# Attention with the value products two steps behind the exponentials, and the row sums directly behind them

## The reference, cut to what matters

```python
q = jnp.dot(x, Wq).reshape(b, t, H, HD).transpose(0, 2, 1, 3)
scores = jnp.einsum('bhqd,bhkd->bhqk', q, k)
scores = jnp.where(causal[None, None], -jnp.inf, scores)
weights = jax.nn.softmax(scores * (1.0 / HD ** 0.5), axis=-1)
ctx = jnp.einsum('bhqk,bhkd->bhqd', weights, v)
```

## Time and profile before

| | us |
|---|---|
| median of 3 runs | 3003.71 (2999.08 to 3004.33) |
| the profiled execution | 2999.23 |
| its span in the profile | 2997.6 |
| first and last score matmul of the attention (L475) | 360.1 and 1307.8 |
| PE busy, share of the span | 96% |
| DVE, POOL and ACT busy | 43%, 32%, 30% |

### The profile page before, as it was taken

The page is one execution under the profiler, slowest core; times in us unless marked ns, Lnnn a source line. Parts: engine busy times, 40 slices in busy tenths (PEclk is TensorE's granted clock), DMA queues, the critical chain, the costliest instruction groups (busy, mean ns, idle before and its releaser), DMA issues. The chain is left out here.

```text
span 2997.6 us, 43157 instructions
## 1 busy us (share of the span) xinstructions
PE 2863.8 (96%) x17688; PEld 1233.8 (41%) x17688; DVE 1275.0 (43%) x1579; ACT 896.9 (30%) x1599; POOL 969.7 (32%) x553
## 2 busy tenths in 40 slices
PE   6999799999999999989959999999999998999998
PEld 3445333333333333224434444444444444444443
DVE  5334877777877877125642232232233220001001
ACT  3111166666666666740111111121111110000000
POOL 0000066766767667742222222222222221001001
PEclk9999799999999999999979999999999999999999
DMA  4222101011011010022221111111111113223320
GB/s 163 79 74 76 41 1 42 2 42 42 1 42 33 10 28 1 1 78 95 101 56 39 39 45 42 42 41 40 42 42 45 39 34 114 66 66 93 104 66 28
DMA packets 146158, 152.58 MB, mean 51 GB/s; under 512 B 44912, under 2 KB 121200, under 8 KB 146032
## 3 DMA queue, kind: packets, MB, share of 16 engines
q1 hardware_dynamic: 146032, 150.78, 16.7%
HBM read 100.80 MB, written 49.81 MB: 50 GB/s over the span
## 5 line engine op out<-in xcount | busy, mean ns | idle before, releaser
L681 POOL TENSOR_TENSOR c_prob<-c_prob 128x1024 f32<-128x1024 f32 (+1 forms) x288 | 605.1, 2121 | 583.0 <-ACT c_prob L585 579.9
L602 DVE TENSOR_REDUCE c_maxes<-c_s 128x2 f32<-128x1024 f32 (+3 forms) x640 | 648.7, 1059 | 219.8 <-PE c_s L456 113.6
L585 ACT ACTIVATE c_prob<-c_s 128x512 f32<-128x512 f32 (+1 forms) x1152 | 598.0, 571 | 371.8 <-PE c_s L475 187.9
L475 PE MATMUL c_s<-c_q,c_k 97*128 97x512 f16 (+3 forms) x1280 | 365.4, 353 | 8.2 <-DMA c_q<-c_mrow 2.7
L1086 DVE SCALAR_TENSOR_TENSOR e_h<-e_up,e_silu 128x512 f32<-128x512 f32 (+1 forms) x88 | 60.8, 691 | 579.8 <-PE e_up L1048 579.8
L490 PE MATMUL c_ctx<-c_prob,v_sb 128*32 128x512 f32 (+3 forms) x2560 | 294.1, 540 | 0.5 <-ACT c_c L574 0.5
L1135 POOL TENSOR_TENSOR e_hl<-e_h,e_hh 128x512 f16<-128x512 f32 (+1 forms) x88 | 101.9, 1158 | 588.8 <-ACT e_hh L1109 588.8
L1046 PE MATMUL e_gp<-x_hi,e_w_hi 128*128 128x512 f16 (+1 forms) x704 | 267.7, 380 | 2.5 <-DVE e_w_lo L1076 2.5
L1047 PE MATMUL e_gp<-x_lo,e_w_hi 128*128 128x512 f16 (+1 forms) x704 | 267.7, 380 | 0.0
L1048 PE MATMUL e_gp<-x_hi,e_w_lo 128*128 128x512 f16 (+1 forms) x704 | 267.6, 380 | 0.0
L1047 PE MATMUL e_up<-x_lo,e_w_hi 128*128 128x512 f16 (+1 forms) x704 | 266.9, 379 | 0.0
(11 more groups left out here) (141 smaller groups left out, 3212.2 us busy)
## 6 DMA issues: line engine op xcount, KB each, us to landing
h_hi<-e_hh SPq DMA_DIRECT2D x84, 128.0 KB, 1.7
h_lo<-e_hl SPq DMA_DIRECT2D x84, 128.0 KB, 1.8
f_h_hi<-h_hi SPq DMA_DIRECT2D x7, 1344.0 KB, 8.5
f_h_lo<-h_lo SPq DMA_DIRECT2D x7, 1344.0 KB, 6.9
b_x<-L_attn_x SPq DMA_DIRECT2D x16, 512.0 KB, 6.5
c_q<-qk_hi SPq DMA_DIRECT2D x16, 512.0 KB, 6.9
d_x<-L_attn_x SPq DMA_DIRECT2D x16, 512.0 KB, 5.1
x_dram<-d_x SPq DMA_DIRECT2D x16, 512.0 KB, 2.6
```

Source lines behind the costliest of these rows:

```text
L475: last = nc.tensor.matmul(S2[:, h % 2, at:at + w], K[:, g % 2, k * P:(k + 1) * P], Q[:, g % 2, h, b * BANK + q:b * BANK + q + w], start=Tr ...
L585: nc.scalar.activation(prob(g, s, 0, w)[:, h, :], S2[:, h % 2, 0:w], ACT.Exp, scale=exp_scale).then_inc(exp_done, 1)
L602: nc.vector.tensor_reduce(MAXES[:, heads, t, u], S1[:, heads, 0:unit_width(tile)], AX.X, ALU.max).then_inc(maxed, 1)
L681: return nc.gpsimd.tensor_tensor(one, one, two, ALU.add)
```

## The change

Three edits, all in `attend`. Products are issued two steps behind the scores instead of one. The sum pieces of a step are issued directly behind the products, between the two pairs of heads, instead of at the step's end behind the late unit; a piece made from a single step's exponentials gets a wait for these of its own. ScalarE reads a finished context one step later. The close after the last group is reordered to match.

```diff
@@ sums_after
-                    if c is not None:
+                    if c is None:
+                        pe.wait_ge(exp_done, REP * (STEPS * g + a + 1))
+                    else:
                         pe.wait_ge(added, 2 * (len(pairs) * g + pairs.index((a, c))) + half + 1)
@@ order on TensorE
                 for s in range(STEPS):
                     scores(g, s, (0, 1))
-                    if s:
-                        products(g, s - 1)
+                    if s >= 2:
+                        products(g, s - 2)
                     elif g:
-                        products(g - 1, STEPS - 1)
+                        products(g - 1, STEPS + s - 2)
+                    if g:
+                        sums_after(g - 1, s + STEPS)
+                    sums_after(g, s)
                     if more:
                         for tile in early_in[s]:
                             unit(g + 1, tile)
...
-                    if g:
-                        sums_after(g - 1, s + STEPS)
-                    sums_after(g, s)
+            products(GROUPS - 1, STEPS - 2)
+            sums_after(GROUPS - 1, STEPS)
             products(GROUPS - 1, STEPS - 1)
-            for s in range(STEPS, STEPS + 3):
+            for s in range(STEPS + 1, STEPS + 3):
                 sums_after(GROUPS - 1, s)
@@ ScalarE
-                        if s == last_of[b] + 1:
+                        if s == last_of[b] + 2:
                             read_context(g, b)
-                    if g and s == 0:
+                    if g and s == 1:
                         read_context(g - 1, NB - 1)
```

## The result

The changed kernel takes 3075.68 us in the median (3073.37 to 3076.53, 4 runs) against 3004.02 us (2999.08 to 3007.24) before: 1.0239 times, 95% interval 1.0226 to 1.0252, 71.7 us more. 3082 was forecast, with a range of 3058 to 3110.

The account below looks back on a forecast made before the run. TensorE's order bounds steps with units, ScalarE's round those without. Groups 1 to 6 +56 us, group 0 +7, last group +14, close +1.5: together +78 on 3003.7, so 3082 us, range 3058 to 3110.

Parts of the forecast that it names:

- The ordinary step: Attention step with a unit, no mask or seam: 2.97 us would become 3.35, +0.38, 12 times a group.
- the sum piece in the first half: Sum piece moved between head 1's scores and the next head 2's: +0.46 us there, 0.11 saved behind a product.
- The floor of 1.58 us: Second half, head 2's scores to the next head 1's, cannot be shorter: ScalarE's round takes 0.43 + 1.15 us.
- 4 masked steps: Steps with a masked late unit and sum piece; TensorE's order still rules, each gains 0.11 us: -0.4 a group.
- the two seams inside a group: Block changes at steps 8 to 12 and 19 to 23, five sum pieces moved at each: +1.1 us each, +2.2.
- the seam between groups: Steps 33 to 5: nine pieces moved, two waits of 0.3 us, some 2.7 given back: +2.0.
- step 6: Sums wait for GpSimd's first addition, late after cutting the previous group's context: 1.2 us, in groups 1 to 6.
- The clock: Rival: TensorE's waits drop its clock to the lower level in the last group: +75 us, 3157; chance 3%.
- The context's read: ScalarE's read moves a step later; the next block's first products wait 0.3 us for it, ends 0 and 0.6.
- the chain: Rival: GpSimd's additions, released over 0.7 us later than assumed, hold up every pair: +64 us, 3145; chance 4%.
- Edits at nothing: Single-step pieces' wait, ring slots, VectorE's earlier `SUM` and SyncE's loads, all costed at no time.
- That TensorE's order alone decides: Rival: no ScalarE floor in the step, so each saved strip visit gains: 28 us faster, 2976; chance 4%.

Follow-up runs that it names:

- doubling the units: Matmuls of unmasked units in groups 1 to 7 issued twice: kernel before 3040.23 us against 3003.70, changed kernel 3079.45 against 3075.68.
- short exponentials: Exponentials cut to a quarter of their columns, in both kernels: changed kernel 3008.04 us, kernel before 2991.31 us.
- the lag alone: Changed kernel with the sum pieces back at the step's end, products still two steps behind: 3009.88 us, 1.0024 times the kernel before.
- the sums' place alone: Kernel before, products one step behind, with sum pieces directly behind the products: 3078.90 us, 1.0252 times the kernel before.
- the later cut: Changed kernel with GpSimd's cut of the previous group's context one pair later: 3081.53 us, 1.0259 times the kernel before.

## Why the prediction was right

**The reading of the bound.** That TensorE's order alone sets a step with a unit, and ScalarE's round the step without one, stands: doubling the units costs 36.5 us before the change and about 4 after, and short exponentials give back 55 of 72 us.

**The ordinary step.** 3.35 was forecast, 3.32 measured. The term that was mis-sized is the sum piece in the first half: I took 0.46 from a product of 256 columns, within 0.43 to 0.57, and it is 1.43 - 1.00 = 0.43, the lower end, which the two pieces in a row had shown. So a visit saves 0.14 us and not 0.11 in an ordinary step. The floor of 1.58 us held: from the scores of head 2 at 980.60 to head 1 of the next step at 981.68 + 0.88 - 0.38 = 982.18 are 1.58.

**The sum.** From the first exponential of the attention to the end of the last sum piece the trace has 71.8 us more, where 78 was forecast. Group 0 came to +6.4 (forecast 7), groups 1 to 6 together to +50.6 (56), the last group with its close to +14.7 (14 + 1.5). The parts of one of the groups 1 to 4, with a step taken from the first matmul of head 1's scores to that of the next head 1, against the terms of the prediction:

| | forecast, us | measured, us |
|---|---|---|
| 12 ordinary steps | +4.6 | +4.1 |
| 4 masked steps (7, 14, 18, 32) | -0.4 | -1.1 |
| the two seams inside a group | +2.2 | +1.7 |
| the seam between groups | +2.0 | +1.7 |
| step 6 | +1.2 | +1.5 |
| together | +9.6 | +7.9 |

The largest miss is the masked steps: they became 0.23 to 0.38 us shorter, where I had 0.11. In step 32 the second half fell from 2.47 to 1.80 us, that is by the piece's 0.57 and 0.10 more. What the 0.10 is was not tried; the sum piece stood there between masks and scores, and no longer does. A slip in the prediction, 36 x 0.46 = 16.4 where it is 16.6, changes nothing.

Part of the closeness is luck. The clock's two falls are 3.2 us of the 71.8, and no term of the prediction had them; without them the forecast would have been 9 us too high and not 6.

**The context's read.** Forecast as a wait of 0.3 us; it is 0.2, at 31 of 32 blocks, 6.2 us in all, in the changed kernel's waits of products. Part of it would stand under the floor anyway.

**GpSimd.** I put the wait in step 6 at 1.2 us and it is 1.50; nowhere else in groups 0 to 6 do the sums wait for it, so the 0.7 us to spare were real. As a rival it did not become the chain: the changed kernel waits for it 11.1 us in all, 9.0 of them in step 6. With short exponentials, where steps are shorter, it begins to: 4 of the last group's ordinary steps wait for it.

**Edits at nothing.** VectorE was costed at nothing because it has idle time in each step. That was wrong in principle: an operation moved against another engine's can get longer. In the changed kernel the cost stays small (TensorE's units wait 22.5 us for VectorE where they waited 20.6), with the lag alone it is 1.25 us a group.

**The rivals.** That TensorE's order alone decides is ruled out by the 0.88 us scores and shown as its own limit by the short exponentials, where the step does get shorter. The rule of the Trainium skill, "TensorEngine Tiling (Array Packing)", Key Properties, that a mode change drains the engine, agrees with the 0.14 us that one change less saves; a step without the unit or with it was still set by the floor, of which that rule says nothing. The clock did not fall in the last group (1.00). It fell for one stretch in the sixth group, about 2 us behind the end of the 1.5 us wait of step 6 (0.51 in the short row above), and in the seventh; steps 6 and 7 together are 1.6 us longer there than in groups 1 to 4. What the prediction read from the earlier trace rows was too strong: TensorE is busy 4.92 of their 7.00 us, so it waited for 2.1 us and not for most of the time.

## What to carry to other kernels

When two engines hand tiles to and fro through two banks, cut the step at the hand-overs and compare each stretch of the busy engine's order with the round through the other one: work may be moved out of a stretch only down to that round, however much a saved change of arrangement promises. Price every such move per step, since it can gain where masks or other work keep the stretch long and lose where they don't. A change of timing on GpSimd can lengthen VectorE's instructions; look at their durations, not at their idle time.

## What the runs showed that was not expected

VectorE's product of two operands in SBUF (128 x 512, 4 bytes) takes 0.65 us alone and up to 2.60 us, with the lag alone, when GpSimd is adding at the time. The wait is inside its own busy time, so no view of waits names it, and it ends when an addition of GpSimd ends. The Trainium skill has this in "SBUF — State Buffer", Who interferes with whom: a VectorE instruction with two SBUF inputs contends with a GpSimd instruction that reads SBUF, for a pair of ports that the two engines share and that is held exclusively. The runs agree as to the blocking. That two SBUF operands are what makes VectorE need the pair was not tried, but the 32 x 32 transposes of `invert_piece`, which have one operand, take 0.70 to 0.71 us in every trace, beside the additions or not.

The second is that the clock fell to 0.50 for 3.4 us at a time in the middle of groups in which TensorE is otherwise busy. In three kernels the wait of 1.5 us in step 6 stands in all of groups 1 to 6; the clock fell behind it in two of them in the changed kernel, in two with the sums' place alone, and in one with doubled units. Behind the 2.2 us wait of the later cut it fell in all six. In the kernel before, and in every other kernel in which TensorE never waits over 0.75 us in groups 1 to 6, it did not fall in them, but in the changed kernel with short exponentials it fell behind waits of 0.65 us and less as well. So the length of the last wait alone does not decide; what does stays open.
